# Attention heads in one step list on one core: value products by groups of 512 queries instead of 256, one query buffer, and a new order of the side steps

## What is computed

```python
qc = layernorm(x @ W_cq, q_norm_w, q_norm_b)                 # 192 wide
q_nope, q_pe = split((qc @ W_q) by 16 heads, 128, 64)
k_pe, kv = split((x @ W_ckv) by 16 heads, 64, 128)
k_nope, v = split(layernorm(kv, kv_norm_w, kv_norm_b) @ W_kv, 128, 128)
q, k = concat(q_nope, rope(q_pe)), concat(k_nope, rope(k_pe))
attn = softmax(causal(q @ k.T / sqrt(192))) @ v              # per head
io = small attention over 8 tokens per index head, chosen by top_k of x @ W_ig   # one row per pair
out = concat_heads(attn + io) @ W_o
x = layernorm(x + out)
out = layernorm(x + (silu(x @ Wu) * (x @ Wg)) @ Wd)          # ternary weights
```

## Time and profile before

| | us |
|---|---|
| median of three runs | 681.37 (680.0 to 683.07) |
| the profiled execution | 678.62 |
| its span in the trace | 676.8 |
| PE busy / DVE busy / ACT busy / POOL busy | 641.9 / 459.8 / 399.7 / 371.4 |
| mean granted clock of TensorE | 0.989 of 2.4 GHz |

### The profile page before, as it was taken

How to read it: one execution, slowest core, us unless ns; L and a number is a source line. 1 busy time by engine, 2 the same in 40 slices (tenths; PEclk the granted TensorE clock), 3 DMA queues, 4 the chain that set the end, 5 groups by cost and what they waited for, 6 DMA issues and landing times.

```text
span 676.8 us, 14055 instructions
## 1 busy us (share of the span) xinstructions
PE 641.9 (95%) x4456; PEld 582.9 (86%) x4456; DVE 459.8 (68%) x1259; ACT 399.7 (59%) x934; POOL 371.4 (55%) x331
## 2 busy tenths in 40 slices
PE   8899999999999999999999999999999999989996
PEld 5777988899889988898889898998899887879895
DVE  4886367666766767666857586667667677997664
ACT  4885337754775475656574658447654758545652
POOL 6873278454745474366728373638454735440664
PEclk9989989999999999999999999999999999899998
DMA  7306231510461037103521244105510384000001
GB/s 232 121 2 158 61 91 38 130 57 1 107 152 54 0 93 163 48 6 93 124 54 38 70 95 91 54 6 118 132 54 0 93 223 111 10 1 1 1 17 47
DMA packets 23551, 49.85 MB, mean 74 GB/s; under 512 B 3168, under 2 KB 16352, under 8 KB 21600
## 3 DMA queue, kind: packets, MB, share of 16 engines
q1 hardware_dynamic: 22144, 47.82, 27.6%
q10 hardware_dynamic: 1376, 1.64, 0.8%
HBM read 16.94 MB, written 1.05 MB: 27 GB/s over the span
## 4 chain that ended last, share of the span: by engine, by line
PE 58%; DVE 14%; ACT 13%; issue 9%; POOL 4%; DMA 1%; ACTq 0%; DVEq 0%; POOLq 0%; SPq 0%
PE J L839 5%; PE J L841 4%; PE J L840 4%; PE J L872 4%; ACT Pb L1164 4%; PE J L885 4%; PE J L888 4%; ACT kvraw L1259 3%; PE J L884 3%; DVE SC L1374 3%; PE SC L859 3%; PE SC L862 3%; PE SC L860 3%; PE SC L863 3%; PE SC L861 3%
## 5 line engine op out<-in xcount | busy, mean ns | idle before, releaser
L1305 DVE TENSOR_TENSOR PTl<-J,PTh 128x512 fp32r<-128x512 f32 (+1 forms) x192 | 102.8, 553 | 66.9 <-ACT PTh L1147 65.8
L1164 ACT ACTIVATE Pb<-SC,nm 128x128 f32<-128x128 f32 (+7 forms) x128 | 95.0, 742 | 56.0 <-DVE nm L1374 55.6
L1374 DVE CUSTOM_DVE_ANT_0 SC<-SC,mask 128x128 f32<-128x128 f32 (+7 forms) x128 | 97.1, 759 | 20.8 <-PE SC L863 19.7
L872 PE MATMUL J<-ident,Pb 128*128 128x128 f32 x576 | 87.8, 278 | 8.9 <-ACT Pb L1164 7.3
L1147 ACT ACTIVATE PTh<-J 128x512 fp32r<-128x512 f32 (+1 forms) x192 | 88.2, 492 | 7.0 <-PE J L872 6.4
L872 PEld LDWEIGHTS J<-ident,Pb 128*128 128x128 f32 x576 | 63.8, 141 | 18.6 <-ACT Pb L1164 8.4
L884 PE MATMUL J<-PTh,Vh 128*128 128x256 f32 x320 | 77.7, 277 | 0.1
L885 PE MATMUL J<-PTh,Vl 128*128 128x256 f32 x320 | 76.0, 284 | 0.0
L859 PE MATMUL SC<-KNh,QNh 128*128 128x128 f32 (+2 forms) x192 | 69.3, 361 | 0.1
L1147 ACT ACTIVATE ATh<-J 128x256 fp32r<-128x256 f32 x64 | 24.5, 383 | 70.5 <-PE J L888 69.6
L862 PE MATMUL SC<-KK,QS 128*128 128x128 f32 (+2 forms) x192 | 65.9, 343 | 0.0
(11 more groups left out here) (304 smaller groups left out, 1894.9 us busy)
## 6 DMA issues: line engine op xcount, KB each, us to landing
KK<-RK SPq DMA_DIRECT2D x30, 512.0 KB, 6.3
QS<-RQh SPq DMA_DIRECT2D x15, 256.0 KB, 7.5
QS<-RQl SPq DMA_DIRECT2D x15, 256.0 KB, 6.6
KX<-KX SPq DMA_DIRECT2D x14, 256.0 KB, 2.4
QX<-QX SPq DMA_DIRECT2D x14, 256.0 KB, 2.4
r_kv<-in_W_ckv SPq DMA_DIRECT2D x7, 384.0 KB, 3.6
r_o<-in_W_o SPq DMA_DIRECT2D x18, 128.0 KB, 2.1
r_qn<-in_W_qT SPq DMA_DIRECT2D x16, 128.0 KB, 2.2
```

The costliest lines, as they stand in the source:

```text
L872: last = pe.transpose(o[:, tile(j - 4 * c)], Pb[i % 2][:, tile(j)], ident[:, :])
L1164: act.activation(Pb[i % 2][:, w], SC[i % 2][:, s], ACT.Exp, bias=nm[:, i % 2:i % 2 + 1], scale=-1.0, accum_out=sm[:, b, i:i + 1]).then_inc ...
L1305: dve.tensor_tensor(o, i, h.bitcast(F32), ALU.subtract).then_inc(done[kind], 1)
L1374: dve.tensor_tensor_reduce(out=SC[i % 2][:, s], in0=SC[i % 2][:, s], in1=mask[:, 128 * (7 - i):S], scale=-SCALE, scalar=HIGH, op0=ALU.add, ...
```

## The change

`pv` works on two groups of 512 queries. Group 0 (tiles 0 to 3) has four diagonal key blocks with 512, 384, 256 and 128 columns; group 1 (tiles 4 to 7) has four blocks of 512 columns and four diagonal ones. `PTh` and `PTl` are laid out by blocks of 128x128 (`key_blocks`), and the folded weights `Wqnh`, `Wqnl` live in a gap of them. `ATh` and `ATl` are one buffer of 512 columns, evicted once per group; `wo` still has four steps per head. The last head (`pv_last`) keeps four groups of 256. `QNh[1]` and `QNl[1]` are the buffers of head parity 0: `qn` waits on ACT until `qk` of tile 4c+3 of the head before is done. Steps stand in new places; the middle pair before:

```diff
+DIAG = [0, 16]
+GAP = 26
+BLOCKS = 29
+
+
+def key_blocks(n):
+    i = TILE_OF[n]
+    g, ii, full = i // 4, i % 4, i >= 4 and n == CH0[i]
+    first, step, nb = (ii, 4, 4) if full else (DIAG[g] + ii, 3, ii + 1)
+    return slice(first, first + step * (nb - 1) + 1, step), nb
...
-        Wqnh, Wqnl = sb("Wqnh", [128, 2, NOPE], F32R), sb("Wqnl", [128, 2, NOPE], F32R)
...
-        QNh.append(sb("QNh1", [128, S], F32R))
-        QNl.append(sb("QNl1", [128, S], F32R))
+        QNh.append(QNh[0])
+        QNl.append(QNl[0])
...
-        PTh, PTl = sb("PTh", [128, T, 256], F32R), sb("PTl", [128, T, 256], F32R)
-        ATh = [sb(f"ATh{i}", [128, 256], F32R) for i in range(2)]
-        ATl = [sb(f"ATl{i}", [128, 256], F32R) for i in range(2)]
+        PTh, PTl = sb("PTh", [128, BLOCKS * 128], F32R), sb("PTl", [128, BLOCKS * 128], F32R)
+        ATh, ATl = sb("ATh", [128, 512], F32R), sb("ATl", [128, 512], F32R)
+        Wqnh, Wqnl = [X[:, 128 * GAP:128 * GAP + 256].rearrange("p (r n) -> p r n", r=2) for X in (PTh, PTl)]
...
-               "vs": 1, "pv": 4, "wo": 4, "side": 13, "tc": NCH, "wb": 1, "rwt": 1, "wtot": 3, "ht": 2}
+               "vs": 1, "pv": 2, "wo": 4, "side": 13, "tc": NCH, "wb": 1, "rwt": 1, "wtot": 3, "ht": 2}
...
-            exp_at = [[2, 2, 2, 2, 2, 2, 2, 2], [2, 2, 2, 2, 2, 2, 2, 2]]
+            exp_at = [[2, 0, 2, 2, 2, 1, 2, 1], [2, 0, 2, 2, 2, 0, 2, 1]]
+            if last:
+                exp_at[1] = [2] * T
             s = []
...
             return [(kind, 0, c) for c in cs]
 
-        PRO_PE = (each("qc", 0, 1, 2, 3) + each("kpe", 0) + each("qc", 4, 5, 6, 7) + each("kv", 0, 1) + each("qm", 0, 1) +
+        PRO_PE = (each("qc", 0, 1, 2, 3, 4, 5) + each("kpe", 0) + each("qc", 6, 7) + each("kv", 0, 1) + each("qm", 0, 1) +
                   each("ab", 0) + each("kpe", 1) + each("qp", 0) + each("qps", 0) + each("qn", 0) + each("kv", 2) +
                   each("kt", 0) + each("kv", 3) + each("qm", 2, 3) + each("wb", 0))
-        PRO_ACT = (each("xs", 0, 1, 2, 3) + each("cs", 0) + each("w0", 0) + each("kpe", 0) + each("qnm", 0) + each("kv", 0, 1) +
+        PRO_ACT = (each("xs", 0, 1, 2, 3) + each("cs", 0) + each("wkvh", 0) + each("w0", 0) + each("kpe", 0) + each("qnm", 0) + each("kv", 0, 1) +
                    each("qm", 0, 1) + each("ab", 0) + each("qnm", 1) + each("kpe", 1) + each("rk", 0) + each("qn", 0) +
                    each("kvn2", 0) + each("kv", 2) + each("kt", 0) + each("rkl", 0) + each("kv", 3) + each("qm", 2))
-        PRO_DVE = (each("xs", 0, 1, 2, 3) + each("qc", 0, 1, 2, 3) + each("w0p", 0) + each("w0", 0) + each("qnm", 0) +
-                   each("w0k", 0) + each("qc", 4, 5, 6, 7) + each("kvs", 0) + each("qms", 1) + each("qm", 0, 1) + each("kvs", 1) +
+        PRO_DVE = (each("xs", 0, 1, 2, 3) + each("qc", 0, 1, 2, 3) + each("wkvl", 0) + each("w0p", 0) + each("qnm", 0) +
+                   each("w0k", 0) + each("w0", 0) + each("qc", 4, 5, 6, 7) + each("kvs", 0) + each("qms", 1) + each("qm", 0, 1) + each("kvs", 1) +
                    each("kvnh", 0) + each("ab", 0) + each("ropeq", 0) + each("qn", 0) + each("rk", 0) + each("kt", 0) +
-                   each("kvs", 2) + each("wb", 0))
-        PRO_POOL = (each("wkp", 0) + each("wkv", 0) + each("qrs", 0) + each("wqpl", 0) + each("rks", 0) + each("qrs", 1) +
+                   each("kvs", 2) + each("qms", 3) + each("kvs", 3) + each("wb", 0))
+        PRO_POOL = (each("wkp", 0) + each("qrs", 0) + each("wqpl", 0) + each("rks", 0) + each("qrs", 1) +
                     each("rkm", 0) + each("kvnh", 0) + each("rks", 1) + each("rkm", 1) + each("rqrows", 0) + each("vsh", 0) +
                     each("kvnh", 1) + [("wqn", 1, 0), ("wosp", 1, 0)])
...
         @blk1.sync
         def _(sp):
-            for c in (0, 2):
+            sp.dma_start(r_cq, W_cqg.rearrange("(k p) n -> p k n", p=128)).then_inc(ld_cq, 16)
+            for c in (1, 3):
                 sp.dma_start(KX[:, :, quarter(c)], xT.rearrange("(k p) n -> p k n", p=128)[:, :, quarter(c)]).then_inc(ld_xt[c], 16)
-                if c == 0:
-                    sp.dma_start(r_cq, W_cqg.rearrange("(k p) n -> p k n", p=128)).then_inc(ld_cq, 16)
...
 
-            gp.wait_ge(ld_cq, 16)
-            gp.tensor_copy(Wcqh[:, :, :], r_cq).then_inc(cq_hi, 1)
             gp.wait_ge(cq_hi, 1)
             gp.tensor_tensor(Wcql[:, :, :], r_cq, Wcqh[:, :, :].bitcast(F32), ALU.subtract).then_inc(cq_ready, 1)
 
@@ -752,6 +765,12 @@
                             gp.wait_ge(thr_ready, w + 1)
                         wait(gp, tern_done, c - 1)
                         gp.tensor_scalar(low[c % 2], raw[w][:, half(j)], nthr[:, w:w + 1], None, ALU.is_lt).then_inc(low_done, 1)
+                    if kind == "rowadd":
+                        gp.wait_ge(done["rwt"], 1)
+                        gp.wait_ge(done["wo"], count("wo", NH - 2, c))
+                        a = acc[:, 2 * c:2 * c + 2, :]
+                        rb = row[:, :].rearrange("p (a n) -> p a n", a=1).to_broadcast([128, 2, D])
+                        gp.tensor_tensor(a, a, rb, ALU.add).then_inc(row_added, 1)
                     if kind == "m":
...
                     pe.wait_ge(rk0_ready[c], 2)
                     pe.wait_ge(rq0_ready, c + 1)
+                if i % 4 == 0 and not first:
+                    pe.wait_ge(done["qn"], count("qn", h, i // 4))
                 if i == 0 and not first:
-                    pe.wait_ge(done["qn"], count("qn", h, 1))
                     pe.wait_ge(done["kt"], count("kt", h, 1))
                     wait(pe, stacked[b], 64 * pair + 64 * b)
...
 
             def pv(h, b, g, o):
                 if isinstance(h, int) and h == 0:
-                    if g % 2 == 0:
-                        pe.wait_ge(done["vs"], g // 2 + 1)
+                    pe.wait_ge(done["vs"], g + 1)
                 elif g == 0:
                     pe.wait_ge(done["vs"], h + 2)
-                parts = [(j, slice(0, 256) if j <= 2 * g else slice(128, 256)) for j in range(2 * g + 2)]
+                if isinstance(h, int) and h == NH - 1:
+                    return pv_last(h, b, g, o)
+                full = [(j, slice(0, 512), slice(512 * j, 512 * j + 512)) for j in range(4 * g)]
+                diag = [(4 * g + r, slice(128 * r, 512), slice(128 * (DIAG[g] + 4 * r), 128 * (DIAG[g] + 3 * r + 4))) for r in range(4)]
+                if g == 1:
+                    pe.wait_ge(hi["tc"], NCH * h + CH0[7] + 1)
+                for j, z, q in full:
+                    mm(o[:, z], lhsT=Vh[b][:, j, :], rhs=PTh[:, q], start=j == 0, stop=False)
+                    mm(o[:, z], lhsT=Vl[b][:, j, :], rhs=PTh[:, q], start=False, stop=False)
+                pe.wait_ge(hi["tc"], NCH * h + CH0[4 * g + 4])
+                for j, z, q in diag:
+                    mm(o[:, z], lhsT=Vh[b][:, j, :], rhs=PTh[:, q], start=j == 0, stop=False)
+                    mm(o[:, z], lhsT=Vl[b][:, j, :], rhs=PTh[:, q], start=False, stop=False)
+                pe.wait_ge(pt_lo, NCH * h + CH0[4 * g + 4])
+                for j, z, q in full + diag:
+                    last = mm(o[:, z], lhsT=Vh[b][:, j, :], rhs=PTl[:, q], start=False, stop=j == 4 * g + 3)
+                return last
+
+            def pv_last(h, b, g, o):
+                s, z, parts = g // 2, 2 * (g % 2), []
+                for j in range(2 * g + 2):
+                    r = j - 4 * s
+                    f = max(z, r)
+                    first = 4 * j + f if r < 0 else DIAG[s] + 3 * r + f
+                    parts.append((j, slice(128 * (f - z), 256), slice(128 * first, 128 * (first + z + 2 - f))))
                 pe.wait_ge(hi["tc"], NCH * h + CH0[2 * g + 2])
-                for j, q in parts:
-                    mm(o[:, q], lhsT=Vh[b][:, j, :], rhs=PTh[:, j, q], start=j == 0, stop=False)
-                    mm(o[:, q], lhsT=Vl[b][:, j, :], rhs=PTh[:, j, q], start=False, stop=False)
+                for j, q, w in parts:
+                    mm(o[:, q], lhsT=Vh[b][:, j, :], rhs=PTh[:, w], start=j == 0, stop=False)
+                    mm(o[:, q], lhsT=Vl[b][:, j, :], rhs=PTh[:, w], start=False, stop=False)
                 pe.wait_ge(pt_lo, NCH * h + CH0[2 * g + 2])
-                for j, q in parts:
-                    last = mm(o[:, q], lhsT=Vh[b][:, j, :], rhs=PTl[:, j, q], start=False, stop=j == 2 * g + 1)
+                for j, q, w in parts:
...
-                    pe.wait_ge(hi["pv"], count("pv", u, c))
+                    part = c if isinstance(u, int) and u == NH - 1 else c // 2
+                    pe.wait_ge(hi["pv"], count("pv", u, part))
                     for t in range(2):
-                        z, ah, al = slice(256 * t, 256 * t + 256), ATh[c % 2][:, tile(t)], ATl[c % 2][:, tile(t)]
-                        mm(o[:, z], lhsT=ah, rhs=ABh[b][:, 256:512], start=True, stop=False)
-                        mm(o[:, z], lhsT=ah, rhs=ABl[b][:, 256:512], start=False, stop=False)
```

(27 more changed lines are left out.)

114 lines of the change are left out of this document (64 added, 50 removed).

## The result

The changed kernel takes **672.34 us** (median of 4 runs, 671.41 to 672.95); the kernel before took 680.71 beside it. The profiled execution took 671.9 us with a span of 670.0, against 676.8 before: 6.8 us of span, 18 forecast. Five more runs of the same kernel gave 671.06 and a ratio of 0.986 (0.9839 to 0.9881).

A forecast was written before the change was run, and what follows sets the result against it. TensorE, its matmuls filling 95% of the span, was taken as the bound. Terms -6 -6 -4 -2 = -18 us took the profiled 678.6 to 660.6; with 2.75 for the median, 663.4 us, range 657 to 670.

The forecast's parts named there:

- Part 1: Wider `pv` products, 36 matmuls a head in place of 60, in 15 heads: -6.0 us (-4.5 to -7.7).
- third rival: The width of `pv` brings nothing, matmuls cost by columns alone: 669.4 us, chance 0.10.
- Part 2: Step order within the six middle pairs: about -2.5 recovered, +1.5 new, taken as -1.0 us a pair, -6.0.
- Part 3: One query buffer in place of two: the added ACT wait holds nothing up beyond PE's own order, 0 us.
- Part 4: Prologue and first pair, with the `Wcql` cast and side steps moved: -4.0 us (-7 to +1).
- The first stage: Prologue: TensorE's first real product waits 1.5 us for `Wcql`; moving the cast from POOL to DVE gives -1.0.
- side.10: First pair, near 88 us: a wait and slow clock costing 3.1 us go as the step moves later; counted -2.5.
- The first pair may open another gap: First pair: allowance for a new gap, for which the 3.1 us gain at `side.10` was counted as -2.5.
- Part 5: Last pair: `wo` leaves from ahead of the minimum and `pv` from ahead of `exp`: -2.0 us (-4 to +2).
- POOL's additions: Last pair: four row additions of 512 columns move from DVE to POOL, price unknown; part returns as a wait at `tern`.
- second rival: A new wait in slots 2 and 3 of each pair slows the clock: 691 us, chance 0.10.
- first rival: The waits only move: Part 2 gives 0, Part 4 and Part 5 give half, 672 us, chance 0.18.

The follow-up runs named there:

- narrow: The changed kernel with each attention product split again into matmuls of at most 256 columns, 60 a head in place of 36: 676.72 us, ratio 0.9952.

## Why the prediction was right or wrong

The forecast was -18 us; 8.4 came by the medians and 6.8 between the two profiles. By these, parts 1 to 3 brought -9.8 of -12, and parts 4 and 5 brought +3.1 of -6. So the prediction failed in two steps of its working: head 0 stood in part 4's sum with a gain of 0.5 and no cost, and part 5 took the new order of the last pair for a gain. Both are taken up below.

**Part 1** (-6.0) was right, in size and in kind: 36 matmuls a head, a long product of 4.65 us and a short one of 1.86, together 6.51, between the two estimates of 6.39 and 6.60. In the middle that saves 0.36 a head (13.72 to 13.01 a pair), and taking the width away costs 0.39 to 0.41, so -5.3 to -6.2 over 15 heads. The third rival (columns alone) is refuted, and so are the 0.9 us in all by the formula of the Trainium skill ("TensorE: Matmul & The Clock Gate", Back-to-back issue gap). The prediction left out that this section gives its formula for an isolated matmul only. For a stream of weight loads and matmuls it states about 81 ns at 128 columns and 131 ns at 512; the first agrees with the 85 measured here, the second does not with 232. The pitches read from the rows were the right source.

**Part 2** (-6.0) had its mechanism right and its net too large: the middle brought 8.6 less 4.3 to 4.7 for `pv`, so -3.9 to -4.3, or -0.65 to -0.72 a pair. "About -2.5 recovered, +1.5 new" a pair is measured as 2.2 recovered (1.33 by `exp` ahead, 0.86 by `qn.1` late) and 1.3 to 1.5 new. That the 2.5 was nearly met is in part luck: the gains that the text names add up to 1.6 to 1.8 (0.8 to 1.0, 0.5 and 0.33). Its places were partly wrong. I credited the boundary of the earlier trace rows to `wo1.1` leaving slot 6. The run that moved `qn.1` alone got that boundary's 0.86 with `wo1.1` where it was. Of the feared hold-ups, `kt.1` behind `kvn2` waits less than before (0.3 for 0.75), and the new cost is in small pieces that the wait list does not name.

**Part 3** (0): no wait was added, right. But its sentence "the ACT wait added holds nothing up" stopped at the wait. The buffer forces `qn.1` into slot 7, and that move is worth 0.86 a pair. I used it in part 2 without seeing that it needs nothing else of the change.

**Part 4** (-4.0; by the profiles about +0.5). Two of its terms were mis-sized with opposite signs. The first stage was given -1.0 "of a 1.5 us wait". It brings about 3, since the wait is 1.5 to 2.5 and the clock behind it mostly drops. That part of the error is that one profile, the luckiest of six, was taken for the rule. `side.10` came as priced between the two profiles (-3.1, with the clock at 1.00 in the changed kernel), but only the wait of 1.4 is there each time; the 1.7 of slow clock came in two of five kernels, and so that half of the price is luck. What sank the part is head 0, which I had given no cost: -0.5 was put on moving the side steps, and +3.6 came. TensorE is idle 7.4 us there, where it was 5.4 with the 1.4 of `side.10` in it. 1.2 to 1.9 of the loss is the new order; the rest is not settled. "The first pair may open another gap" was there as half a microsecond, and the gap was 1.5; `exp5` behind the eviction again gives 0.7 of it back.

**Part 5** (-2.0, came as +2.6) failed in the step "takes `pv` from ahead of `exp`". I checked what left the place ahead of `exp`, and not what `exp` was now ahead of. In this slot alone a `tern` stands first, so the same number in `exp_at` puts `exp7` ahead of the queries' eviction, whose bank the next transposes want. One entry changed gives 1.1 to 1.3 back. Some 0.9 more of the loss goes with a slow stretch of the clock in the last head, which is missing in two kernels with the same last pair; what brings it is open. The named risk, POOL's additions, was real on DVE (1.77 for 0.74 us) and cost nothing.

The second rival, a wait that takes the clock along, did happen, but at the two ends and not in the pairs. The first rival's time (672) was met by luck: it gives nothing to the order within a pair, which brought 3.9, and -3 to parts 4 and 5, which brought +3.1.

**Open:** 1.7 to 2.4 us of head 0's 3.6; why a slow stretch of the clock follows the same wait in some kernels and not in others; why the wait for `Wcql` takes 1.5 us in one kernel and 2.5 in another; and which step makes each small piece of the two long places' cost.

## What to carry to other kernels

In list-driven kernels a step moved for one reason changes what it covers: test each move alone, since here two free reorderings (1.33 and 0.86 us a pair) were worth more than the restructuring that carried them, which gave 0.8 by its width and cost 1.3 to 1.5 by its places. Ends need their own look, slot by slot, at what stands behind each moved `exp` on every engine's queue; a position counted in steps means something else where one list has an extra step. And price a wait outside a loop from several profiles, since the clock behind it may fall or not: near the start that doubled the price in some.

## What the runs showed of the hardware

The same first stage, in the profiles of six kernels, waited 1.5 to 2.5 us for the same data, and from 8 to 16 us the mean clock was 1.00 (wait of 1.5), 0.79 (1.7 to 2.0) or 0.57 (2.5) of 2.4 GHz. With the 1.4 to 3.2 us by which their first scores then came later this could make up much of the spread of the old kernel (677 to 683 us), but of that kernel one run alone has a profile, so it isn't shown. At `side.10` waits of 1.39 to 1.44 us in five kernels were followed by a clock of 0.72 over 6 us twice, and of 1.00 three times.

Matmuls of 512, 256 and 128 columns follow each other every 0.23, 0.12 and 0.085 us at full clock, so one of 128 costs more than half of one of 256. In `narrow`, 24 splits a head cost 0.39 us, 16 ns each on average. While POOL added two 128x512 operands (1.3 us), a 0.74 us VectorE operation took 1.77.
